# Attention block on one core: one split of the second weights moved ahead of the group mean, and a wait put ahead of GpSimd's first sums of rows

## The chip, the cores and the metric

One core of one Trainium2 chip runs one program. The metric is device microseconds of that core, the median of three runs. The profile that is read here is one further execution of the same program; times on the trace count from its first instruction.

## The reference, cut to what matters

The input x is (16, 512, 32, 32): 16 images of 512 channels and N = 1024 positions. For each image

```
h   = group_norm(x) * w + b             # 32 groups of 16 channels
q, k, v = split(qkv_w @ h + qkv_b)      # 512 x 1024 each
attn = softmax(q^T k / sqrt(512))       # 1024 x 1024
out  = x + out_w @ (attn v)^T + out_b
```

The kernel uses that q^T k = h^T (wq^T wk) h and that out_w v = (out_w wv) h. So two products of weights are made once, ahead of all images: G from wk and wq ("weights 0"), U from wv and the transposed out_w ("weights 1"). The biases become three vectors of weights: sums over rows of the weights, each row scaled by a bias.

## The kernel before, in words

All matrices are kept as two float32r parts: a high part, rounded by ScalarE, and a "rest" (the small part), the full value less the high part, made by VectorE. A product is three matmuls: high by high, high by rest, rest by high (lines 459 to 461 in the main part; 475, 482 and 484 for the products of weights). Each engine runs an order that is written out by hand, and engines meet at semaphores only; nothing is planned at run time. So an instruction that waits holds everything that stands behind it on its own engine.

After the start, 16 images follow one another, each with a T stage (G by h), the scores, a V stage (h by U) and the output. TensorE has work nearly without a gap. The change is in the start alone, the first 35 us or so:

- **SP's queue** issues the loads in this order: weights 0 in four blocks (each block is 128 rows of two matrices, two transfers of 256 KB), the first image in four transfers of 512 KB, the matrix `block_avg` for the group means, then weights 1 in four blocks (lines 344 to 356).
- **ScalarE** makes the high parts (`weight_part`, line 749) of weights 0, then scales the rows of weights 0 by the biases (`wq_wk_rows`, line 774), makes the high parts of blocks 0 and 1 of weights 1, copies G out of PSUM (`product_part`, line 754) and makes block 2's high part. Then it waits for the scale and bias of the group norm (`s_norm`, 8 steps) and makes the high parts of h for two channel tiles (line 757), block 3's high part, and the other two of h. Then come rows of weights 1 scaled (line 785), `first_full(2)` (line 761), which waits for the sum of the scaled rows (`s_rows_sum[0]`), two more rows, U out of PSUM, and `first_full(3)`, which also waits for TensorE's first two weight vectors.
- **VectorE** makes the rests (`weight_rest`, line 1216), the statistics of the first image (lines 1230, 1235), four small steps after the mean (lines 1239 to 1244), one step after the variance (line 1248), three steps that give scale and bias (lines 1252 to 1256), the rests of G and U (`product_rest`, line 1221), and h in full and its rests (lines 1316, 1264). Then follow the combined tiles of h, the key bias's dot products and the tiles of T (lines 1279 to 1373).
- **TensorE** runs the product of weights 0, six matmuls of zeros (line 504), the group mean (line 492), the first high by high part of weights 1 (three tiles; the fourth needs a bank that is still read), the variance (line 516, after VectorE's fourth small step), the low parts of block 0, and so on to block 3. Then comes the T stage, with the weight vectors (line 466) behind its first nine matmuls.
- **GpSimd** adds the scaled rows of weights 0 with accumulating transfers, SBUF to SBUF, 512 KB each: the even blocks (line 1109) and the odd blocks (line 1111) as soon as ScalarE has scaled them, then, behind the step for the reciprocal root of the variance (line 1121), the sum of both (line 1116). The same follows for weights 1.

At the start of the first image's scores, ScalarE makes the eight high parts of the T sums (line 834), of which the last two need VectorE's last T sums (line 1373, `first_sum(S4, kk)`), and then copies the first score tiles (`copy_first`, line 869). TensorE's second scores product waits for the first of these copies (`s_p1`).

Semaphores that matter: `s_w[w][k]` (block k of weights w landed, 32 for both transfers), `s_whi`, `s_wlo` (high part, rest made), `s_norm` (steps of the norm), `s_even`, `s_odd`, `s_rows_sum` (sums of rows).

Of the kernel before, what the change touches and what calls it, by code (L numbers as in the profile page):

```python
# [19 lines left out]
CT = C // P  # L20
# [3 lines left out]
DMA = 16  # L24
# [85 lines left out]
def attention_kernel(nc, x, wq, wk, wv, wo_t, cols, block_avg, out):  # L110
# [5 lines left out]
    with ctx:  # L116
# [3 lines left out]
        def sem(name):  # L120
            return ctx.enter_context(nc.semaphore(name))
# [75 lines left out]
        def g_rows(t, i):  # L197

            return t[:, i // 2:i // 2 + 3:2, i % 2, :]
# [65 lines left out]
        u_bank = [4, 5, 6, 3]  # L265
# [3 lines left out]
        s_w = [[sem(f"weights{w}_loaded{k}") for k in range(CT)] for w in range(2)]  # L269
# [59 lines left out]
        def lone_wait(eng, which, count):  # L329
            eng.wait_ge(which, count)  # L330
            eng.sem_inc(s_carrier, 1)
# [124 lines left out]
        def _(pe):  # L456
# [15 lines left out]
            def product_high(w, k, banks, tiles=range(CT)):  # L472
                pe.wait_ge(s_whi[w], k + 1)
                for i in tiles:
                    nc.tensor.matmul(ring[:, banks[i], :], w_hi[w][:, 2 * k, i * P:(i + 1) * P], w_hi[w][:, 2 * k + 1, :],
                                     start=k == 0, stop=False)

            def product_low(w, k, banks, tiles=range(CT)):
                pe.wait_ge(s_wlo[w], k + 1)
                for i in tiles:  # L480
                    cs = slice(i * P, (i + 1) * P)
                    nc.tensor.matmul(ring[:, banks[i], :], w_hi[w][:, 2 * k, cs], w_lo[w][:, 2 * k + 1, :],
                                     start=False, stop=False)
                    a = nc.tensor.matmul(ring[:, banks[i], :], w_lo[w][:, 2 * k, cs], w_hi[w][:, 2 * k + 1, :],
                                         start=False, stop=k == CT - 1)
                    if k == CT - 1:
                        a.then_inc(s_prod[w], 1)

            def first_mean():
                pe.wait_ge(s_avg, DMA)  # L490
                pe.wait_ge(s_aggr, CT)
                nc.tensor.matmul(ps_mean, avg[:, :], mv[:, :, 0], start=True, stop=True).then_inc(s_mean, 1)
# [8 lines left out]
            def zero_products(count):  # L501

                for _ in range(count):
                    nc.tensor.matmul(ring[:, 7, :], zeros[:, 0:P], zeros[:, 0:HALF], start=True, stop=True)
# [4 lines left out]
            for k in range(CT):  # L509
                product_high(0, k, g_bank)  # L510
                product_low(0, k, g_bank)
            zero_products(6)
            first_mean()
            product_high(1, 0, u_bank, range(CT - 1))
            pe.wait_ge(s_norm, 4)
            nc.tensor.matmul(ps_var, avg[:, :], spread[:, :], start=True, stop=True).then_inc(s_var, 1)
            product_low(1, 0, u_bank, range(CT - 1))
            product_high(1, 1, u_bank, range(CT - 1))

            pe.wait_ge(s_prod_lo[0], 1)  # L520
# [575 lines left out]
        def _(pool):  # L1096
# [5 lines left out]
            def rows(w, k):  # L1102
                return raw[0][:, 2 * k:2 * k + 2, :] if w == 0 else wo_rows[k][:, :]

            def add_rows(w):

                sides = 2 - w
                pool.wait_ge(s_rows[w], 2 * sides)
                nc.gpsimd.dma_start(rows(w, 2), rows(w, 0), accum_op=ALU.add).then_inc(s_even[w], DMA)
                pool.wait_ge(s_rows[w], 4 * sides)  # L1110
                nc.gpsimd.dma_start(rows(w, 3), rows(w, 1), accum_op=ALU.add).then_inc(s_odd[w], DMA)

            def sum_rows(w):
                pool.wait_ge(s_even[w], DMA)
                pool.wait_ge(s_odd[w], DMA)
                nc.gpsimd.dma_start(rows(w, 3), rows(w, 2), accum_op=ALU.add).then_inc(s_rows_sum[w], DMA)

            add_rows(0)
            pool.wait_ge(s_warm, 1)
            pool.wait_ge(s_norm, 5)  # L1120
# [84 lines left out]
        def _(dve):  # L1205
# [7 lines left out]
            def weight_rest(w, k):  # L1213
                dve.wait_ge(s_whi[w], k + 1)
                here = slice(2 * k, 2 * k + 2)
                nc.vector.tensor_tensor(w_lo[w][:, here, :], raw[w][:, here, :], w_hi[w][:, here, :].bitcast(FP32),
                                        ALU.subtract).then_inc(s_wlo[w], 1)

            def product_rest(w, i, dst_lo, dst_hi, src):
                dve.wait_ge(s_prod_hi[w], i + 1)  # L1220
                nc.vector.tensor_tensor(dst_lo, src, dst_hi.bitcast(FP32), ALU.subtract).then_inc(s_prod_lo[w], 1)

            def g_rest(i):
                product_rest(0, i, g_rows(g_lo, i), g_rows(g_hi, i), ring[:, g_bank[i], :].rearrange("p (a n) -> p a n", a=2))

            def stats_part(n, q):
                k, half = q // NB, q % NB
                if half == 0:
                    dve.wait_ge(s_x[k], (n + 1) * DMA)
                nc.vector.bn_stats(stats[:, k, half, :], xs[:, k, half * HALF:(half + 1) * HALF]).then_inc(s_stats, 1)  # L1230

            def first_stats_close():
                lone_wait(dve, s_stats, CT * NB)
                for k in range(CT):
                    nc.vector.bn_aggr(mv[:, k, :], stats[:, k, :, :].rearrange("p s e -> p (s e)")).then_inc(s_aggr, 1)

            def first_about_mean():
                dve.wait_ge(s_mean, 1)
                nc.vector.tensor_copy(gmean[:, :], ps_mean).then_inc(s_norm, 1)
                nc.vector.tensor_tensor(dmean[:, :], ps_mean, mv[:, :, 0], ALU.subtract).then_inc(s_norm, 1)  # L1240
                dve.wait_ge(s_norm, 2)
                nc.vector.tensor_tensor(shift[:, :], dmean[:, :], dmean[:, :], ALU.mult).then_inc(s_norm, 1)
                dve.wait_ge(s_norm, 3)
                nc.vector.tensor_tensor(spread[:, :], shift[:, :], mv[:, :, 1], ALU.add).then_inc(s_norm, 1)

            def first_variance():
                dve.wait_ge(s_var, 1)
                nc.vector.tensor_scalar(veps[:, :], ps_var, EPS, None, ALU.add).then_inc(s_norm, 1)
# [9 lines left out]
            def h_rest(n, k):  # L1258
                if n == 0:
                    dve.wait_ge(s_first[k], 1)  # L1260
                else:
                    dve.wait_ge(s_hf, (n - 1) * CT + k + 1)
                dve.wait_ge(s_hhi, n * CT + k + 1)
                nc.vector.tensor_tensor(h_lo[:, k, :], h_full[:, k, :], h_hi[:, k, :].bitcast(FP32),
                                        ALU.subtract).then_inc(s_hlo, 1)
# [45 lines left out]
            def first_full(k):  # L1311

                dve.wait_ge(s_even[0], DMA)
                dve.wait_ge(s_odd[0], DMA)
                dve.wait_ge(s_norm, NORM)
                nc.vector.tensor_scalar(h_full[:, k, :], xs[:, k, :], h_scale[:, k:k + 1], h_bias[:, k:k + 1],
                                        ALU.mult, ALU.add).then_inc(s_first[k], 1)
# [3 lines left out]
            for q in range(CT * NB):  # L1321
                stats_part(0, q)
            first_stats_close()
            first_about_mean()
            weight_rest(1, 0)
            first_variance()
            g_rest(0)
            weight_rest(1, 1)
            first_affine()
            weight_rest(1, 2)  # L1330
            for i in range(1, CT):
                g_rest(i)
            first_full(0)
            weight_rest(1, 3)
            h_rest(0, 0)
            first_full(1)
            h_rest(0, 1)
# [447 lines left out]
```

## Time and profile before

| | us |
|---|---|
| three runs | 1977.72, 1978.09, 1980.64 |
| median | 1978.09 |
| the profiled execution, its own time | 1979.92 |
| its span, first to last instruction | 1978.1 |
| TensorE busy in it | 1971.6 |
| VectorE, ScalarE, GpSimd busy | 1664.6, 1123.1, 448.0 |
| TensorE's granted clock, mean | 1.000 |

The own time of the profiled execution is 1.8 us longer than its span; the rest lies before the first and after the last instruction. TensorE's ends are modelled, so its busy time is a bound, not a proof that it worked at its peak.

### The profile page before, as it was taken

What the parts mean: (1) busy time and instruction counts of PE and PEld (TensorE: products, weight loads), DVE (VectorE), ACT (ScalarE), POOL (GpSimd) and SP (SyncE); (2) the same over time, 40 slices, a digit from 0 to 9 for tenths busy, and PEclk for the clock granted to TensorE, in tenths of its full rate; (3) what the DMA queues carried; (4) which work ended last, traced back from release to release, by engine and by line L of the source; (5) the groups of instructions that cost most, each with busy time, mean ns of one, the idle gap of its engine ahead of it and who ended that gap; (6) DMA issues with size and microseconds to landing.
All of it is one profiled execution on the core that took longest, in us unless ns stands there. A gap on an engine that the chain in (4) does not pass through costs nothing.

```text
span 1978.1 us, 26068 instructions
## 1 busy us (share of the span) xinstructions
PE 1971.6 (100%) x9894; PEld 1681.8 (85%) x9895; DVE 1664.6 (84%) x2010; ACT 1123.1 (57%) x1431; POOL 448.0 (23%) x306
## 2 busy tenths in 40 slices
PE   9999999999999999999999999999999999999999
PEld 7888888888888888888888888888888888888887
DVE  7897997969889798796988979788797988969866
ACT  6564646646465564645746466564664646556461
POOL 1112140221412213131231401214022131221311
PEclk9999999999999999999999999999999999999999
DMA  6305233051431604325043340424305143160411
GB/s 177 129 7 114 75 66 128 7 149 40 75 119 17 172 6 76 119 50 144 6 75 114 58 136 7 112 76 70 124 7 151 37 75 119 21 172 2 75 33 54
DMA packets 102636, 157.89 MB, mean 80 GB/s; under 512 B 49376, under 2 KB 51264, under 8 KB 102512
## 3 DMA queue, kind: packets, MB, share of 16 engines
q0 software_dynamic: 31264, 73.15, 17.1%
q1 hardware_dynamic: 71248, 83.08, 13.7%
q8 instruction: 79, 1.29, 0.3%
q14 instruction: 45, 0.37, 0.1%
HBM read 85.57 MB, written 68.26 MB: 78 GB/s over the span
## 4 chain that ended last, share of the span: by engine, by line
PE 88%; DVE 2%; ACT 1%; issue 0%; DMA 0%; SPq 0%; DVEq 0%; ACTq 0%
PE ring L459 29%; PE ring L460 29%; PE ring L461 29%; DVE stage L1438 0%; DVE stage L1457 0%; DVE run_max L1450 0%; DVE stats L1230 0%; ACT stage L881 0%; DVE stage L1506 0%; DMA u_dram<-r_lo 0%; DVE r_lo L1431 0%; ACT xs L888 0%; ACT ring L869 0%; ACT r_hi L863 0%; DVE u_lo L1518 0%
## 5 line engine op out<-in xcount | busy, mean ns | idle before, releaser
L459 PE MATMUL ring<-r_hi 128*128 128x512 f32 (+1 forms) x1724 | 656.6, 381 | 0.2 <-DVE r_lo L1477 0.2
L460 PE MATMUL ring<-r_lo,r_hi 128*128 128x512 f32 (+1 forms) x1724 | 656.4, 381 | 0.0
L461 PE MATMUL ring<-r_hi,r_lo 128*128 128x512 f32 (+1 forms) x1724 | 656.2, 381 | 0.0
L459 PEld LDWEIGHTS ring<-r_hi 128*128 128x128 f32 x1724 | 324.3, 188 | 62.1 <-DVE r_lo L1477 0.7
L461 PEld LDWEIGHTS ring<-r_hi,r_lo 128*128 128x128 f32 x1724 | 324.2, 188 | 62.1
L460 PEld LDWEIGHTS ring<-r_lo,r_hi 128*128 128x128 f32 x1724 | 324.3, 188 | 61.2
L881 ACT ACTIVATE stage<-ring,keybias 128x512 f32<-128x512 f32 x256 | 175.2, 685 | 164.2 <-PE ring L461 161.4
L1170 POOL PARTITION_ALL_REDUCE stage<-stage x32 | 127.2, 3976 | 466.5 <-DVE stage L1530 466.5
L854 ACT ACTIVATE stage<-ring,by_tile 128x512 f32<-128x512 f32 x120 | 82.5, 688 | 243.8 <-PE ring L461 243.8
L1462 DVE TENSOR_TENSOR r_lo<-stage,r_hi 128x1024 fp32r<-128x1024 f32 x128 | 182.2, 1453 | 0.0
L1450 DVE TENSOR_TENSOR run_max<-run_max,stage 128x512 f32<-128x512 f32 x192 | 132.0, 694 | 55.2 <-ACT stage L881 50.6
L459 PE MATMUL ring<-h_hi,r_hi 128*128 128x512 f32 x444 | 172.8, 389 | 0.1
L461 PE MATMUL ring<-h_hi,r_lo 128*128 128x512 f32 x444 | 172.7, 389 | 0.0
L460 PE MATMUL ring<-h_lo,r_hi 128*128 128x512 f32 x444 | 172.7, 389 | 0.0
L1457 DVE TENSOR_TENSOR stage<-stage,all_max 128x1024 f32<-128x1024 f32 x128 | 151.9, 1229 | 0.0
L900 ACT ACTIVATE stage<-stage 128x1024 f32<-128x1024 f32 x128 | 134.6, 1052 | 18.7 <-DVE stage L1457 18.7
L915 ACT ACTIVATE r_hi<-stage 128x1024 fp32r<-128x1024 f32 x128 | 135.9, 1061 | 2.8 <-DMA u_dram<-r_lo 0.3
L1165 POOL PARTITION_ALL_REDUCE all_max<-run_max x32 | 57.9, 1810 | 304.6 <-DVE run_max L1450 160.2
L761 ACT ACTIVATE stage<-xs,by_tile 128x1024 f32<-128x1024 f32 x62 | 76.5, 1233 | 83.6 <-DMA sum_row<-stage 82.6
L1230 DVE BATCH_NORM_STATS2 stats<-xs 128x6 f32<-128x512 f32 x128 | 80.6, 684 | 46.4 <-DMA xs<-x_in 46.4
L1406 DVE TENSOR_TENSOR stage<-stage,ring 128x512 f32<-128x512 f32 x90 | 60.6, 686 | 69.0 <-PE ring L461 58.9
L767 ACT ACTIVATE r_hi<-stage 128x1024 fp32r<-128x1024 f32 x64 | 68.0, 1063 | 76.8 <-DVE stage L1279 72.3
(199 smaller groups left out, 3924.5 us busy)
## 6 DMA issues: line engine op xcount, KB each, us to landing
xs<-x_in SPq DMA_DIRECT2D x64, 512.0 KB, 5.8
out<-xs SPq DMA_DIRECT2D x60, 512.0 KB, 2.7
out<-run_max POOLq DMA_DIRECT2D x60, 256.0 KB, 5.7
inv<-inv_row SPq DMA_DIRECT2D x32, 256.0 KB, 4.5
out<-spare POOLq DMA_DIRECT2D x30, 256.0 KB, 7.6
out<-all_max POOLq DMA_DIRECT2D x30, 256.0 KB, 5.0
r_hi<-g_dram POOLq DMA_DIRECT2D x15, 512.0 KB, 6.3
r_lo<-g_dram POOLq DMA_DIRECT2D x15, 512.0 KB, 5.7
```

The source lines that it names most:

```text
L459: nc.tensor.matmul(ps_out, st_hi, m_hi, start=first, stop=False, skip_group_check=goes_on)
L460: nc.tensor.matmul(ps_out, st_hi, m_lo, start=False, stop=False, skip_group_check=goes_on)
L461: return nc.tensor.matmul(ps_out, st_lo, m_hi, start=False, stop=last, skip_group_check=goes_on)
L854: nc.scalar.activation(stage[:, to + kk, :], ring[:, T_BANK[p] + kk, :], ACT.Identity, bias=t_bias[:, i:i + 1]).then_inc(done, 1)
L881: nc.scalar.activation(stage[:, to, :], ring[:, bank + i, :], ACT.Identity, bias=keybias[:, m:m + 1]).then_inc(done, 1)
L900: nc.scalar.activation(here, here, ACT.Exp, scale=SCALE).then_inc(s_exp, 1)
L915: nc.scalar.activation(p_pair(r_hi, b, nb, q), stage[:, 8 * nb + 2 * q:8 * nb + 2 * q + 2, :], ACT.Copy).then_inc(s_phi, 1)
L1170: nc.gpsimd.partition_all_reduce(stage[:, 8 * nb + 1, :], stage[:, 8 * nb, :], P, bass.bass_isa.ReduceOp.add).then_inc(s_allsum, 1)
L1230: nc.vector.bn_stats(stats[:, k, half, :], xs[:, k, half * HALF:(half + 1) * HALF]).then_inc(s_stats, 1)
L1450: nc.vector.tensor_tensor(run_max[nb][:, :], first, stage[:, 8 * nb + m, :], ALU.max).then_inc(s_rmax[nb], 1)
L1457: nc.vector.tensor_tensor(here, here, all_max[:, :].rearrange("p (o n) -> p o n", o=1).to_broadcast([P, 2, HALF]), ALU.subtract).then_inc( ...
L1462: nc.vector.tensor_tensor(p_pair(r_lo, b, nb, q), stage[:, 8 * nb + 2 * q:8 * nb + 2 * q + 2, :], p_pair(r_hi, b, nb, q).bitcast(FP32), AL ...
```

## The change

TensorE: two of six matmuls of zeros go; the low parts of block 0 of weights 1 are moved ahead of the wait for VectorE's fourth small step and of the variance. GpSimd: a wait for block 2 of weights 1 is put ahead of the first two sums of rows. VectorE: the rest of block 0 of weights 1 is moved ahead of the steps after the mean, the first rest of G ahead of the variance's step, and the rest of block 3 ahead of `first_full(0)`.

```
-            zero_products(6)
+            zero_products(4)
             first_mean()
             product_high(1, 0, u_bank, range(CT - 1))
+            product_low(1, 0, u_bank, range(CT - 1))
             pe.wait_ge(s_norm, 4)
             nc.tensor.matmul(ps_var, avg[:, :], spread[:, :], start=True, stop=True).then_inc(s_var, 1)
-            product_low(1, 0, u_bank, range(CT - 1))
             product_high(1, 1, u_bank, range(CT - 1))
...
+            pool.wait_ge(s_w[1][2], 2 * DMA)
             add_rows(0)
             pool.wait_ge(s_warm, 1)
             pool.wait_ge(s_norm, 5)
...
             first_stats_close()
+            weight_rest(1, 0)
             first_about_mean()
-            weight_rest(1, 0)
+            g_rest(0)
             first_variance()
-            g_rest(0)
             weight_rest(1, 1)
             first_affine()
             weight_rest(1, 2)
             for i in range(1, CT):
                 g_rest(i)
+            weight_rest(1, 3)
             first_full(0)
-            weight_rest(1, 3)
             h_rest(0, 0)
```

## Rows read from the trace of the kernel before

**Rows 1.** The page, busy us of each engine, share of the span, instructions.

```profile
PE 1971.6 (100%) x9894; PEld 1681.8 (85%) x9895; DVE 1664.6 (84%) x2010; ACT 1123.1 (57%) x1431; POOL 448.0 (23%) x306
```

**Rows 2.** Timeline of TensorE: start us, us, engine, line, op, tiles, count [idle before, releaser].

```profile
19.32 1.24 PE L504 MATMUL ring<-spare 128*128 128x512 bf16 x5
20.39 0.28 PE L492 MATMUL ring<-inv 128*128 128x4 f32 x2
20.54 0.96 PE L475 MATMUL ring<-r_hi 128*128 128x512 f32 x3
21.39 0.39 PE L516 MATMUL ring<-inv 128*128 128x4 f32 x2
22.53 0.50 PE L482 MATMUL ring<-r_lo,r_hi 128*128 128x512 f32 x1 [0.75 <-DVE r_lo L1216]
...
34.90 1.84 PE L466 MATMUL ring<-inv,stage 128*128 128x1 f32 x16
```

**Rows 3.** Timeline of VectorE, from the mean to the T sums.

```profile
20.71 0.16 DVE L1239 COPY inv<-ring 128x4 f32<-128x4 f32 x1 [2.70 <-PE ring L492]
...
21.26 1.22 DVE L1216 TENSOR_TENSOR r_lo<-stage,r_hi 128x1024 fp32r<-128x1024 f32 x1
22.39 0.15 DVE L1248 TENSOR_SCALAR inv<-ring 128x4 f32<-128x4 f32 x1
...
23.06 1.22 DVE L1216 TENSOR_TENSOR r_lo<-stage,r_hi 128x1024 fp32r<-128x1024 f32 x1
24.19 0.16 DVE L1252 TENSOR_TENSOR by_tile<-inv,col 128x4 f32<-128x4 f32 x1
...
28.31 1.22 DVE L1216 TENSOR_TENSOR r_lo<-stage,r_hi 128x1024 fp32r<-128x1024 f32 x1
...
38.11 1.23 DVE L1264 TENSOR_TENSOR h_lo<-stage,h_hi 128x1024 fp32r<-128x1024 f32 x1 [1.02 <-ACT stage L761]
...
60.37 1.41 DVE L1373 SCALAR_TENSOR_TENSOR stage<-ring,by_tile,stage 128x512 f32<-128x512 f32 x2
```

**Rows 4.** Timeline of ScalarE, from the second weights to the first score copies.

```profile
17.09 1.06 ACT L749 ACTIVATE r_hi<-stage 128x1024 fp32r<-128x1024 f32 x1 [0.76 <-DMA stage<-wo_t]
18.45 1.06 ACT L749 ACTIVATE r_hi<-stage 128x1024 fp32r<-128x1024 f32 x1 [0.30 <-DMA stage<-wo_t]
...
24.78 2.38 ACT L757 ACTIVATE h_hi<-xs,by_tile 128x1024 fp32r<-128x1024 f32 x2 [2.37 <-DVE by_tile L1256]
27.07 1.04 ACT L749 ACTIVATE r_hi<-stage 128x1024 fp32r<-128x1024 f32 x1
...
31.50 1.23 ACT L761 ACTIVATE stage<-xs,by_tile 128x1024 f32<-128x1024 f32 x1
...
36.84 1.24 ACT L761 ACTIVATE stage<-xs,by_tile 128x1024 f32<-128x1024 f32 x1 [0.96 <-PE ring L466]
...
62.37 2.04 ACT L869 ACTIVATE ring<-ring 128x512 f32<-128x512 f32 x4
```

**Rows 5.** Timeline of GpSimd.

```profile
9.21 0.19 POOL L1100 TENSOR_TENSOR inv<-by_tile 128x4 f32<-128x4 f32 x1 [8.38 <-issue]
...
22.70 1.06 POOL L1121 TENSOR_TENSOR inv<-inv,by_tile 128x4 f32<-128x4 f32 x1 [5.19 <-DVE inv L1248]
26.08 0.91 POOL L1116 DMA_DIRECT2D stage<-stage  x1 [2.32 <-DMA stage<-stage]
```

**Rows 6.** DMA issues from 10.1 to 11.05 us: size, us to landing.

```profile
stage<-wo_t SPq DMA_DIRECT2D x1, 256.0 KB, 10.6
```

**Rows 7.** DMA issues from 26 to 27 us: the last sum of rows.

```profile
stage<-stage POOLq DMA_DIRECT2D x1, 512.0 KB, 4.6
```

**Rows 8.** Windows: us, busy (count) of PE, PEld, DVE, ACT, POOL, granted clock, DMA share, GB/s.

```profile
14.20:19.20 5.00, 5.00 (x23) 3.96 (x23) 3.67 (x10) 3.94 (x6) 2.04 (x2) 1.00 1.06 379
19.20:24.20 5.00, 4.18 (x20) 2.89 (x19) 3.42 (x9) 3.21 (x6) 1.06 (x1) 1.00 1.06 223
```

**Rows 9.** Timeline of TensorE's weight loads at the second scores product.

```profile
63.07 0.19 PEld L459 LDWEIGHTS ring<-h_hi,r_hi 128*128 128x128 f32 x1 [0.47 <-DVE r_lo L1379]
```

More of the change, by code:

```diff
@@ L511, in _ @@
                 product_low(0, k, g_bank)
-            zero_products(6)
+            zero_products(4)
             first_mean()
             product_high(1, 0, u_bank, range(CT - 1))
+            product_low(1, 0, u_bank, range(CT - 1))
             pe.wait_ge(s_norm, 4)
             nc.tensor.matmul(ps_var, avg[:, :], spread[:, :], start=True, stop=True).then_inc(s_var, 1)
-            product_low(1, 0, u_bank, range(CT - 1))
             product_high(1, 1, u_bank, range(CT - 1))
@@ L1116, in sum_rows @@
                 nc.gpsimd.dma_start(rows(w, 3), rows(w, 2), accum_op=ALU.add).then_inc(s_rows_sum[w], DMA)
+            pool.wait_ge(s_w[1][2], 2 * DMA)
             add_rows(0)
@@ L1323, in _ @@
             first_stats_close()
+            weight_rest(1, 0)
             first_about_mean()
-            weight_rest(1, 0)
+            g_rest(0)
             first_variance()
-            g_rest(0)
             weight_rest(1, 1)
@@ L1332, in _ @@
                 g_rest(i)
+            weight_rest(1, 3)
             first_full(0)
-            weight_rest(1, 3)
             h_rest(0, 0)
```

## The prediction

> **What bounds the kernel now.** The page comes first: TensorE is busy 1971.6 us [rows 1] of a span of 1978.1, so the time can only fall by idle time or by work that leaves TensorE, and only where TensorE, followed to the end, starts everything earlier. The change touches the start alone, so I read the start engine by engine. TensorE's timeline [rows 2] has one place worth having: the six matmuls of zeros (five records; the sixth is missing, they run from 19.09 to 20.37, so 0.213 each), the mean at 20.39, three matmuls from 20.54, the variance at 21.39, and the first low part only at 22.53, released by VectorE's rest of block 0. VectorE [rows 3] sat idle 2.70 us for the mean, from 18.0 to 20.71, and made that rest at 21.26, after the mean's steps, though ScalarE had the high part at 18.15 (17.09 and 1.06) [rows 4]. The order is the cause, not the work.
>
> The next question is where a gain could be lost again. ScalarE waits 2.37 us for the scale and bias, to 24.78; GpSimd's root (22.70, 1.06 us) is part of that chain [rows 4, 5]. Then ScalarE runs without idle time to `first_full(3)` at 36.84, which waited 0.96 us for the weight vectors, started at 34.90; VectorE waited for it to 38.11 and has no idle time from there to 60.37 and beyond [rows 2 to 4]. Its last T sums there release ScalarE's last high part and the copy at 62.37, and TensorE's weight load at 63.07 stood 0.47 us [rows 9]. The row names line 1379, which TensorE doesn't wait for in the code; the wait that the code has is on the copy of 62.37. This is the second place that decides: TensorE's gain in the first 35 us is cut there to what ScalarE and VectorE gain.
>
> **TensorE, part by part.** A 512-column matmul costs 0.227: 23 of them touch 5.0 us, 22 pitches [rows 8].
> - Two zeros fewer: 2 x 0.213 = 0.43. The mean moves from 20.39 to 19.96. Its input is ready at 18.0, so no wait opens.
> - The low parts of block 0, six matmuls, follow the three high ones: 20.11 + 9 x 0.227 = 22.15. Their rest is made at 18.2 to 19.4 (VectorE is idle then), in time and ahead of the mean. The variance comes behind them at 22.15, where its input is ready at about 20.9, and takes about 0.15 like the mean. So the 0.17 of waiting at 21.22 to 21.39, the 1.0 from there to 22.53, and about 0.1 of restart go. The gain behind the variance is 0.43 + 0.17 + 1.0 + 0.1 = 1.7.
> - The seven matmuls to block 1's low parts end at 22.30 + 7 x 0.227 = 23.89 (the bank they need is free: the first rest of G now ends at 21.5). The weights want to load at 23.66.
>
> **VectorE and the norm.** The copy of the mean follows TensorE's row by 0.32, so the variance is read at 22.15 + 0.32 = 22.47, against 22.39 [rows 2, 3]: hardly moved, because before it stood behind the rest of block 0. The rest of block 1 starts at 22.55 and not at 23.06, and is seen at 23.8, where TensorE wants it at 23.66; the restart hides all but 0.03. The root starts 0.31 after the variance, at 22.78, and ends at 23.84 [rows 5]. Before, the three affine steps began at 24.19 since VectorE was busy until then; now it is free at 23.7 and the root ends it: about 24.0. **So the norm's end, and ScalarE from 24.78 on, gain only 0.2** (bounds 0.05 to 0.3, by how soon VectorE sees the root, which no row shows).
>
> Block 3's high part on ScalarE goes from 27.07 to 26.88, and its rest starts when that is done, at 27.97 and not 28.31, since `first_full(0)` no longer stands ahead. It is seen at 29.24; TensorE wants it at 29.14, and again the restart hides it. Without this edit TensorE would have stood 0.4 or more. Price on VectorE: the rests of h for tiles 0 to 2 come some 0.4 later at first, 31.1 for tile 0, where TensorE wants 30.95: under 0.05. The product of weights 1 ends near 31.2, and the weight vectors stand at 33.25 against 34.90, a gain of 1.65.
>
> **The second place.** `first_full(3)` needs the vectors (36.84 - 1.65 = 35.2) and ScalarE's own queue: it stood idle 0.96 before 36.84, and as neighbours overlap by some 0.1 it could have started at 35.74, now 35.55. So it gains 1.29, not 1.65. VectorE's own queue gives the same (its copies behind U's rests end at 36.8). VectorE goes from 38.11 to 36.8 and carries 1.3 through to 60.37; TensorE's third k step wants this rest at about 38.95 and gets it at 38.1. ScalarE's last high part there is due by VectorE's sum, not by its own queue, so TensorE is released at 63.07 - 1.3. Behind that point everything depends on work that moved by 1.3, and is carried along.
>
> **GpSimd's wait.** Behind it stand both sums, the root, the last sum, then all of GpSimd. Before, block 2 of weights 1 landed at 21.2 (issued at 10.6 and 10.6 more) [rows 6], beside sums that were issued as soon as ScalarE had scaled the rows (it was through at 16.33, 0.76 ahead of 17.09 [rows 4]). Blocks 0 and 1 came at 17.09 and 18.45 [rows 4], so block 2 is at most 1.36 later, 19.8, if nothing delays it; taking out the sums' bytes until then (I estimate 0.28 MB at 379 GB/s, 0.7 us [rows 8]) gives 19.1. Bounds: 18.3, and 21.2 as before. For the release I allow 0.5, and about 1 us for each issue like the 0.91 of 26.08 [rows 5]: 19.6 to 21.7, ahead of the root's 22.78, so the root pays nothing. The last sum took 4.6 to land [rows 7]; its 0.52 MB at 223 GB/s [rows 8] are 2.35 of that, 2.25 lie before and behind. Both sums are 1.05 MB, 4.7 us: landed at 19.6 + 4.7 + 2.25 = 26.5. The last sum is issued at about 26.8, where it was 26.08, and lands at 31.4. ScalarE wants it at 31.3 (31.50 - 0.2) [rows 4], TensorE at 33.25. Price 0.1, bounds 0 and 2.2. What it gives back: block 3, due on ScalarE at 26.9, has slack either way. I value the wait at nothing for TensorE.
>
> By the Trainium skill (DMA: Bandwidth & Descriptors, Anatomy of one DMA, SWDGE path) a transfer costs 2.0 us and its bytes at 436 GB/s, an estimate of 3.2 us for 512 KB; the row says 4.6 [rows 7], and by the page the last sum would land near 30 with no price at all.
>
> **Sum.** -1.3 + 0.1 = -1.2 us. Against the profiled execution's own 1979.92 this is 1978.7. That execution is 1.8 above the median of the runs; the same sum on the median 1978.09 gives **1976.9**.
>
> **The rivals.**
> 1. *Slower: GpSimd's wait ends late.* For: block 2 did land at 21.2, and nothing in the profile proves that the sums caused it. Then the sums are issued at 21.7 to 23.8, the root ends near 24.8 (affine steps 0.7 later than before), both sums land at 28.6, and the last sum lands at 33.5. ScalarE's `first_full(2)` goes to 33.5 (+2.0), `first_full(3)` to 37.7, and VectorE's chain and TensorE at 63.07 by +0.9: 1979.0. It decides from a last sum later than about 32.6, that is block 2 after 20.3. Against: DMA moved 379 GB/s while three blocks of weights and both sums shared it.
> 2. *The sums slip by half a microsecond or so*, block 2 near 19.7: 32.0, gain cut to 0.6: 1977.5.
> 3. *The root is held by VectorE.* Now it would start 0.23 into a rest of two SBUF inputs (22.55 to 23.77); before it began beside a rest of G that reads PSUM. The same engine's 128x4 add took 0.19 at 9.21, the root 1.06 [rows 5], so part of it may already be such waiting, or the power itself. If held to 23.77, the root ends at 24.8, the affine steps are 0.7 later than before, and TensorE stands 1.0 for block 3's rest; `first_full(3)` goes to 36.44: gain 0.4, 1977.7. The Trainium skill has this rule (SBUF — State Buffer, Who interferes with whom: a VectorE instruction with two SBUF inputs contends with a GpSimd one that reads SBUF, and the first issued holds the shared port). Before, the root ended at 23.76 beside such an instruction from 23.06, but had begun first, so the trace doesn't contradict it.
> 4. *Nothing binds at 63.07*: VectorE's chain has slack that I don't see, and TensorE carries 1.65: 1976.4.
> 5. *The change doesn't do what it says*: the wait doesn't speed blocks 2 and 3, which have slack anyway. Same time as my forecast.
>
> **How the numbers follow.** A measurement of this kernel can tell about 0.2%, 4 us, from no change; three equal runs of before spread over 2.9. Chances: forecast (with rival 5) 0.60, slip 0.13, root held 0.11, slower by 0.9 us 0.08, 1.65 carried 0.08. The range takes in 1976.4 and 1979.0 and about 1 us of scatter below and 0.5 above: 1975.4 to 1979.5. Every case lies within 4 us, so faster by over 0.2% gets 0.03, slower 0.03, what is left 0.94; these small chances stand for something not thought of, such as a lower granted clock, of which the profile shows none (1.00 in both windows [rows 8]).
>
> **What the profile after would show.** Mean at 19.96; rest of block 0 at 18.2 on VectorE; no TensorE idle before line 482; variance read at 22.5; affine steps at 24.0; block 3's rest at 28.0; weight vectors at 33.25; last sum issued near 26.8 and `first_full(2)` at 31.3 to 31.5; `first_full(3)` at 35.6; the copy of 62.37 at 61.1 and the weight load of 63.07 at 61.8, still with idle time before it. I am wrong if affine steps start after 24.5 (rival 3), if `first_full(2)` waits for DMA by more than 0.5 (rivals 1, 2), or if the load of 63.07 comes at 61.4 (rival 4).

## The result, and the profile after

The change made the kernel slower: 1981.24 us (median of 22 runs) against 1978.16 (22 runs), ratio 1.0015, interval 1.001 to 1.0021. That is 3.1 us, outside my range, and clear of noise: with this many runs the measurement tells about 1 us, not the 4 us that the prediction allowed it. One run of each kernel took far longer (2166.11 before, 4020.49 after) and is left out of the ratio. The profiled execution took 1981.37, span 1979.6. So the spans of the two profiles (1978.1 and 1979.6) differ by 1.5 only, and half of the loss is not in them. The first experiment finds the other half.

VectorE's timeline of the kernel after, where it answers to [rows 3]:

```profile
18.14 1.22 DVE L1217 TENSOR_TENSOR r_lo<-stage,r_hi 128x1024 fp32r<-128x1024 f32 x1 [0.15 <-ACT r_hi L749]
19.28 0.15 DVE L1240 COPY inv<-ring 128x4 f32<-128x4 f32 x1
...
21.22 0.16 DVE L1249 TENSOR_SCALAR inv<-ring 128x4 f32<-128x4 f32 x1 [0.56 <-PE ring L517]
21.30 1.21 DVE L1217 TENSOR_TENSOR r_lo<-stage,r_hi 128x1024 fp32r<-128x1024 f32 x1
23.47 0.16 DVE L1253 TENSOR_TENSOR by_tile<-inv,col 128x4 f32<-128x4 f32 x1 [0.96 <-POOL inv L1122]
...
28.99 0.81 DVE L1317 TENSOR_SCALAR stage<-xs,by_tile 128x1024 f32<-128x1024 f32 x1 [0.34 <-DMA stage<-stage]
...
39.61 1.23 DVE L1265 TENSOR_TENSOR h_lo<-stage,h_hi 128x1024 fp32r<-128x1024 f32 x1
```

The rest of block 0 stands where the change puts it, at 18.14, and the affine steps begin at 23.47, earlier than the 24.19 of [rows 3]. But the rest of h's last tile, 38.11 there, is at 39.61: +1.5, as the span.

ScalarE's and GpSimd's timelines after, answering to [rows 4] and [rows 5]:

```profile
24.06 2.38 ACT L757 ACTIVATE h_hi<-xs,by_tile 128x1024 fp32r<-128x1024 f32 x2 [1.71 <-DVE by_tile L1257]
...
34.05 1.24 ACT L761 ACTIVATE stage<-xs,by_tile 128x1024 f32<-128x1024 f32 x1 [3.17 <-DMA stage<-stage]
...
38.33 1.25 ACT L761 ACTIVATE stage<-xs,by_tile 128x1024 f32<-128x1024 f32 x1
...
20.07 1.18 POOL L1109 DMA_DIRECT2D stage<-stage  x1 [10.59 <-DMA stage<-wo_t]
20.96 1.20 POOL L1111 DMA_DIRECT2D stage<-stage  x1
21.54 1.90 POOL L1122 TENSOR_TENSOR inv<-inv,by_tile 128x4 f32<-128x4 f32 x1
29.43 0.92 POOL L1116 DMA_DIRECT2D stage<-stage  x1 [5.99 <-DMA stage<-stage]
```

The loss of this profile starts in two rows. The last sum of rows is issued at 29.43, not 26.08, and `first_full(2)` stands 3.17 us for it, to 34.05, which is 2.55 later than in [rows 4]. U's copies and `first_full(3)` stand behind it in ScalarE's queue, and VectorE behind those. The wait of 0.96 that stood ahead of `first_full(3)` before, and about 0.1 of overlap, take up part of it; what is left is the 1.5 of `first_full(3)` (38.33 against 36.84).

The DMA issues of the two first sums after (the even sum, then the odd one), and the DMA by windows with the columns of [rows 8]. The last two numbers of such a line are the busy share of the DMA engines and GB/s:

```profile
stage<-stage POOLq DMA_DIRECT2D x1, 512.0 KB, 4.9
...
stage<-stage POOLq DMA_DIRECT2D x1, 512.0 KB, 7.9
```

```profile
20.00:22.00 2.00, 2.00 (x11) 1.70 (x10) 1.44 (x3) 2.00 (x4) 1.94 (x3) 1.00 0.19 39
22.00:24.00 2.00, 2.00 (x10) 1.60 (x10) 0.98 (x5) 0.35 (x1) 1.44 (x2) 1.00 1.06 197
24.00:26.00 2.00, 2.00 (x11) 1.64 (x10) 2.00 (x4) 1.94 (x2) 0.00 (x0) 1.00 1.03 199
26.00:28.00 2.00, 2.00 (x9) 1.39 (x8) 1.54 (x3) 2.00 (x3) 0.00 (x0) 1.00 0.55 102
```

The even sum landed at 20.07 + 4.9 = 25.0, the odd one at 20.96 + 7.9 = 28.9. Between the last load and the first bytes of the sums the DMA engines were nearly idle: their share was 0.19 from 20 to 22 us, and 0.00 from 20.5 to 21.5. The sums alone moved 198 GB/s. Two more profiles below show the same 2 us, first the kernel before, run once more, then the kernel after with the wait on block 1; there the engines had no gap:

```profile
20.00:22.00 2.00, 1.25 (x5) 1.05 (x6) 2.00 (x4) 2.00 (x4) 1.06 (x1) 1.00 1.05 241
```

```profile
20.00:22.00 2.00, 2.00 (x12) 1.66 (x11) 1.45 (x3) 2.00 (x4) 1.27 (x2) 1.00 0.98 198
```

TensorE after, answering to [rows 2], and the windows in which its granted clock (the third number from the end) isn't 1.00:

```profile
18.13 0.36 PE L492 MATMUL ring<-inv 128*128 128x4 f32 x2
18.34 0.95 PE L475 MATMUL ring<-r_hi 128*128 128x512 f32 x3
19.41 0.50 PE L482 MATMUL ring<-r_lo,r_hi 128*128 128x512 f32 x1
...
20.91 0.28 PE L517 MATMUL ring<-inv 128*128 128x4 f32 x2
...
34.16 1.92 PE L466 MATMUL ring<-inv,stage 128*128 128x1 f32 x16 [0.66 <-DMA stage<-stage]
...
37.18 0.59 PE L461 MATMUL ring<-h_hi,g_lo 128*128 128x512 f32 x1
37.57 0.63 PE L459 MATMUL ring<-h_hi,g_hi 128*128 128x512 f32 x1
```

```profile
36.00:38.00 2.00, 2.00 (x9) 1.59 (x9) 1.52 (x3) 2.00 (x5) 0.86 (x1) 0.80 0.00 0
38.00:40.00 2.00, 2.00 (x6) 1.62 (x5) 2.00 (x6) 1.58 (x2) 0.00 (x0) 0.50 0.76 131
40.00:42.00 2.00, 2.00 (x9) 1.54 (x9) 1.98 (x2) 0.00 (x0) 0.86 (x1) 0.84 0.01 4
```

The mean is at 18.13, not at the 19.96 that I forecast; line 482 still starts about 0.4 late (at 19.41, where three matmuls from 18.34 end at 19.0), since the rest of block 0 is made from 18.14 to 19.36. TensorE stands for the last sum too (0.66), and behind that wait the granted clock falls to half (1.2 GHz) for some three microseconds. At the second scores product TensorE stood again for the copies, 0.59 us, so this half clock seems to have cost nothing at the end; the wait alone, below, lost as much at full clock.

### The profile page after: what moved, and what is told of

It is laid out like the page before. It is cut to its first block, busy times and chain, and to the rows that moved or that the text cites. A ratio compares the mean times of both kernels' runs of the same rounds, so it can differ in the third digit from the quotient of the medians.

```text
span 1979.6 us, 26065 instructions
## 1 busy us (share of the span) xinstructions
PE 1972.5 (100%) x9892; PEld 1680.9 (85%) x9893; DVE 1666.5 (84%) x2010; ACT 1123.3 (57%) x1431; POOL 448.7 (23%) x306
## 4 chain that ended last, share of the span: by engine, by line
PE 88%; DVE 2%; ACT 1%; issue 0%; DMA 0%; SPq 0%; DVEq 0%; ACTq 0%
PE ring L459 29%; PE ring L461 29%; PE ring L460 29%; DVE stage L1439 0%; DVE stage L1458 0%; DVE run_max L1451 0%; DVE stats L1231 0%; ACT stage L881 0%; DVE stage L1507 0%; DMA u_dram<-r_lo 0%; DVE r_lo L1432 0%; ACT xs L888 0%; ACT ring L869 0%; ACT r_hi L863 0%; DVE u_lo L1519 0%
## 5 line engine op out<-in xcount | busy, mean ns | idle before, releaser
L900 ACT ACTIVATE stage<-stage 128x1024 f32<-128x1024 f32 x128 | 134.6, 1052 | 18.6 <-DVE stage L1458 18.6
L915 ACT ACTIVATE r_hi<-stage 128x1024 fp32r<-128x1024 f32 x128 | 135.8, 1061 | 2.8 <-DMA u_dram<-r_lo 0.3
L1151 POOL DMA_DIRECT2D r_hi<-u_dram x15 | 8.6, 572 | 457.4 <-PE ring L461 457.4
```

Of the source, the lines that this page charges most:

```text
L900: nc.scalar.activation(here, here, ACT.Exp, scale=SCALE).then_inc(s_exp, 1)
L915: nc.scalar.activation(p_pair(r_hi, b, nb, q), stage[:, 8 * nb + 2 * q:8 * nb + 2 * q + 2, :], ACT.Copy).then_inc(s_phi, 1)
```

## The experiments

Each time is a median of 10 or 11 runs, beside the kernel before on the same chip. Ratios have intervals of about 0.0009 either way, so the traces carry the finer differences.

**The kernel before, once more.** No edit.

> The kernel before once more, unchanged, for a second profile of it. Theory 1 (the profiled execution of before was not the typical one: TensorE ran at 1.2 GHz to 10.4 us there): the typical execution is at 2.4 GHz from about 7 us, the product of the first weights ends near 17 us, the mean is at about 18.3, the last sum of rows is issued at 26 and lands at 30.7, and ScalarE's first_full(2) waits for it. Span about 1976.4, time 1978.2. Rival: the profile of before was typical and the 1.8 us lie outside the span; then the mean is at 20.4 again.

1978.13 us, ratio 1.0 (0.9991 to 1.0009), span 1976.5. VectorE, ScalarE and GpSimd in this profile:

```profile
21.28 1.21 DVE L1216 TENSOR_TENSOR r_lo<-stage,r_hi 128x1024 fp32r<-128x1024 f32 x1
22.41 0.15 DVE L1252 TENSOR_TENSOR by_tile<-inv,col 128x4 f32<-128x4 f32 x1
...
36.49 1.23 DVE L1264 TENSOR_TENSOR h_lo<-stage,h_hi 128x1024 fp32r<-128x1024 f32 x1
...
30.92 1.25 ACT L761 ACTIVATE stage<-xs,by_tile 128x1024 f32<-128x1024 f32 x1 [0.38 <-DMA stage<-stage]
...
14.01 1.17 POOL L1109 DMA_DIRECT2D stage<-stage  x1 [4.18 <-ACT stage L774]
16.43 0.87 POOL L1111 DMA_DIRECT2D stage<-stage  x1 [1.25 <-ACT stage L774]
20.92 1.06 POOL L1121 TENSOR_TENSOR inv<-inv,by_tile 128x4 f32<-128x4 f32 x1 [3.62 <-DVE inv L1248]
26.32 0.92 POOL L1116 DMA_DIRECT2D stage<-stage  x1 [4.34 <-DMA stage<-stage]
```

The profile that I predicted from was not the typical execution. Here are two of its rows of TensorE, in the product of the first weights, and below them two rows from the same stretch of the profile after:

```profile
7.84 0.63 PE L482 MATMUL ring<-r_lo,r_hi 128*128 128x512 f32 x1
8.27 0.63 PE L484 MATMUL ring<-r_hi,r_lo 128*128 128x512 f32 x1
```

```profile
7.21 0.40 PE L484 MATMUL ring<-r_hi,r_lo 128*128 128x512 f32 x1
7.45 0.40 PE L482 MATMUL ring<-r_lo,r_hi 128*128 128x512 f32 x1
```

There TensorE went at the pace of the 1.2 GHz level (0.43 a matmul) up to 10.4 us, though the granted clock of that stretch reads 1.00; in the others it goes at 0.23 from 7 us or so on. So the mean was 1.8 us late there (20.39 against 18.6), and the weight vectors too (34.90 against 33.12), while the last sum was not (issued at 26.08 and 26.32). This delay hid that ScalarE is bound by the last sum: typically `first_full(2)` waits for it, 0.38 us, to 30.92. In [rows 4] it started at 31.50 without a wait. From here on, "typical" means this second profile.

**The change without GpSimd's wait.**

```
-            pool.wait_ge(s_w[1][2], 2 * DMA)
             add_rows(0)
```

> The kernel after without GpSimd's wait; both new orders of TensorE and VectorE stay. Theory 1 (the 3 us are the wait's: it delays the sums of rows, and ScalarE and VectorE with them): last sum issued near 26.1, landed 30.7, time as before, 1978.2 (ratio 0.9995 to 1.0003), since the last sum binds ScalarE in before too. Rival 2 (the new orders cost, by the root held beside the rest of block 1, or by the restart of TensorE): 1979.5 or more. My prediction's sum, if nothing of the sums bound: 1977.

1978.14, ratio 0.9999 (0.9991 to 1.0008), span 1976.4; last sum issued at 26.22, `first_full(2)` at 30.83. The new orders of TensorE and VectorE neither gain nor cost anything that these runs can tell; what TensorE gains ends at the same sum (`first_full(2)` waits 0.23 for it). Two rows of TensorE at block 3:

```profile
27.16 1.20 PE L475 MATMUL ring<-r_hi 128*128 128x512 f32 x4
28.42 0.50 PE L482 MATMUL ring<-r_lo,r_hi 128*128 128x512 f32 x1
```

TensorE reached block 1's high part 1.48 us sooner than in the typical before (20.76 against 22.24), but this block's low part only 0.85 sooner (28.42 against 29.27): it waited for the high part and for the rest, both behind the norm.

**The wait alone, in the kernel before.**

```
+            pool.wait_ge(s_w[1][2], 2 * DMA)
             add_rows(0)
```

> The kernel before with GpSimd's wait alone. Theory 1: as slow as after, 1981.2 (ratio 1.0013 to 1.0018), last sum issued near 29.4 and landed near 34.0. Rival 2 (the orders cost): 1978.2 to 1979.

1981.03, ratio 1.0015 (1.0006 to 1.0023), span 1979.2; last sum issued at 29.09, `first_full(2)` at 33.72. The wait is the whole loss, within the interval. The clock stayed at 1.00 in every window to 41 us of this profile, so the half clock of the profile after isn't the cause either.

**The wait on another block.** First block 1, as in the diff, then block 3, in place of block 2.

```
-            pool.wait_ge(s_w[1][2], 2 * DMA)
+            pool.wait_ge(s_w[1][1], 2 * DMA)
```

> The kernel after with the wait on block 1 of the second weights, not block 2. Block 1 landed near 18.4, block 2 near 19.9. Theory 1: the sums are issued 1.5 us earlier, so about half of the loss comes back: 1979.7 (1979.2 to 1980.3). Rival 2: no change against after, 1981.2. A third possibility, that the sums' landing is set by the DMA engines and not by the issue: 1981.2 too, with the odd sum landing at 28.9 again.

1978.95, ratio 1.0003 (0.9994 to 1.0012), span 1977.3.

> The kernel after with the wait on block 3 of the second weights, the last load, in place of block 2. So far first_full(2) on ScalarE starts with the landing of the last sum: 30.8 us without a wait, 31.8 with block 1, 34.0 with block 2, and the span follows it one for one. Theory 1: block 3 lands about 1.1 later than block 2, the sums and the span come 0.5 to 1.3 later: 1982.3. Rival (the loss has another cause, such as the half clock seen in after): 1981.2, as after.

1982.31, ratio 1.0021 (1.0012 to 1.003), span 1980.5. With these the loss follows the place of the wait (the last column is what is left of the span after VectorE begins the rest of h's last tile):

| kernel | even sum issued | last sum issued | `first_full(2)` | rest of h's last tile | span | span less that rest |
|---|---|---|---|---|---|---|
| before, typical | 14.01 | 26.32 | 30.92 | 36.49 | 1976.5 | 1940.0 |
| wait on block 1 | 18.59 | 27.19 | 31.80 | 37.37 | 1977.3 | 1939.9 |
| wait alone, block 2 | 19.74 | 29.09 | 33.72 | 39.28 | 1979.2 | 1939.9 |
| after, block 2 | 20.07 | 29.43 | 34.05 | 39.61 | 1979.6 | 1940.0 |
| wait on block 3 | 20.96 | 30.33 | 34.96 | 40.52 | 1980.5 | 1940.0 |

The kernel ends 1939.9 to 1940.0 us after VectorE begins this rest in every profile of this study; the first profile of before (38.11, 1978.1) has the same. Block 1 cost less than I expected: the even sum started 4.6 us later, and the last sum was issued 0.9 later. In the typical before the first two sums were in flight for 8.6 and 9.4 us, beside the loads; issued at 18.59 and 19.48 they took 4.9 and 7.2, and the DMA engines went from the loads to the sums with hardly a gap. From block 1 to the kernel after the even sum's issue moves by 1.48 and the last sum by 2.24, and from there to block 3 both move by 0.9, while the engines stand idle in between (from 20.5 to 22.5 us for block 3). Starting the sums late costs little as long as the engines stay busy, and one for one or more behind the loads.

**The queue behind the sum.** The kernel after, with the work behind `first_full(2)` moved ahead of it:

```
             wo_rows_part(2)
-            first_full(2)
             wo_rows_part(1)
             wo_rows_part(3)
             for i in range(CT):
                 product_part(1, i, u_hi[:, i, :], ring[:, u_bank[i], :])
+            first_full(2)
             first_full(3)
...
             h_rest(0, 1)
-            h_rest(0, 2)
             for i in range(CT):
                 product_rest(1, i, u_lo[:, i, :], u_hi[:, i, :], ring[:, u_bank[i], :])
+            h_rest(0, 2)
```

> The kernel after, with the two rows of weights and U's four copies on ScalarE ahead of first_full(2), and U's four rests on VectorE ahead of the rest of h's third tile. Theory 1 (the price is what stands behind first_full(2) in ScalarE's queue while it waits for the last sum): ScalarE works through its wait, first_full(3) starts near 36.0 in place of 38.3, and most of the loss comes back: 1978.5 to 1979.3. Rival (TensorE's own waits and its half clock in after make the 3 us): 1981.0.

The profile did about as expected: span 1977.1, `first_full(3)` at 35.90, now waiting for TensorE's vectors, and VectorE's rest at 37.17.

```profile
33.77 1.24 ACT L761 ACTIVATE stage<-xs,by_tile 128x1024 f32<-128x1024 f32 x1
35.90 1.24 ACT L761 ACTIVATE stage<-xs,by_tile 128x1024 f32<-128x1024 f32 x1 [0.89 <-PE ring L466]
```

The median did not: 1980.84, ratio 1.0013 (1.0004 to 1.0022), which is the rival's number. The eleven runs fall in two groups. Four with a mean granted clock of 1.000 took 1978.9 to 1979.75; seven with 0.998 or 0.999 took 1980.68 to 1982.05. The profiled one is the fastest of the first group. So the expected size about holds for runs at full clock, and a lower clock goes with 1.5 us more by the medians of the groups (1980.89 against 1979.36). In the kernel after, runs with 1.000 and 0.999 took the same time, so there ScalarE may hide it. No trace shows an execution of the second group; that its clock fell at the same place as in the profile after is inferred, and what makes it fall stays open: the profile here has the same waits of TensorE as the one of after (0.46 and 0.66 against 0.41 and 0.66) and kept the full clock.

**The same moves in the kernel before.** The diff is the same.

> The kernel before with the same two moves. In its typical execution first_full(2) waits 0.38 for the sum, VectorE 0.77 and 0.48 behind it. Theory 1: a gain of 0.4 to 0.6 us, 1977.6. Rival (TensorE needs the rest of h's third tile sooner than it comes): 1978.5 or more.

1978.14, ratio 0.9999 (0.999 to 1.0008), span 1976.6: no gain, against my theory. `first_full(2)` no longer waits, but `first_full(3)` now stands 0.50 for TensorE's vectors, and VectorE's rest is at 36.56 as before. The next limit was right behind, about as early as the old one.

**The root beside another instruction.** The change without the wait, and

```
-            g_rest(0)
             first_variance()
+            g_rest(0)
             weight_rest(1, 1)
```

> The kernel after without GpSimd's wait, and on VectorE the first rest of G behind the variance's step again, so that this rest, which reads PSUM, and not block 1's, which reads SBUF twice, stands beside the root on GpSimd. Theory (the root is held by a VectorE instruction that began earlier and reads SBUF twice): the root takes 1.06 us and not 1.90, the affine steps start near 22.5. Rival (it is slow because of the descriptors that GpSimd writes at the time): 1.9 again. Time 1978.1 either way, as the last sum still binds.

Time 1977.96, ratio 0.9999 (0.999 to 1.0008), span 1975.8; the affine steps began at 22.54, as expected. That span is 0.7 under the typical one, but the last sum bound here too (`first_full(2)` waited 0.28); in this execution it was issued at 25.73, 0.6 sooner, as the first sums started 0.3 sooner and flew 0.4 us less. The median shows 0.2, inside the interval. The root in three kernels: without the wait (with VectorE's rest of block 1 ahead of it), this one, and the wait alone on before:

```profile
21.02 1.22 DVE L1216 TENSOR_TENSOR r_lo<-stage,r_hi 128x1024 fp32r<-128x1024 f32 x1
21.26 1.90 POOL L1121 TENSOR_TENSOR inv<-inv,by_tile 128x4 f32<-128x4 f32 x1 [4.07 <-DVE inv L1248]
```

```profile
21.05 1.06 POOL L1121 TENSOR_TENSOR inv<-inv,by_tile 128x4 f32<-128x4 f32 x1 [4.02 <-DVE inv L1248]
```

```profile
21.20 1.98 POOL L1122 TENSOR_TENSOR inv<-inv,by_tile 128x4 f32<-128x4 f32 x1
```

Where VectorE's rest of block 1 began before the root, the root ended 0.91 to 0.93 after that rest's end: 23.16 against 22.24 without the wait, 23.18 against 22.27 with the wait alone, 23.44 against 22.51 in after. Where the root began first, it took 1.06. In the first of the three GpSimd issued no transfer near it (the last at 16.32), so the descriptors aren't the cause there. This is the rule of the Trainium skill (SBUF — State Buffer, Who interferes with whom: a VectorE instruction with two SBUF inputs and a GpSimd one that reads SBUF contend, whoever issues first has the port for the whole instruction). For the root behind the rest these traces agree with it. They show no sign of the other direction: the rest that began at 21.28 in the typical before, 0.36 into the root, took 1.21 as elsewhere.

The run with the wait on block 3 shows a second way to a long root, which I had not looked for:

```profile
20.92 1.22 DVE L1217 TENSOR_TENSOR r_lo<-stage,r_hi 128x1024 fp32r<-128x1024 f32 x1
...
21.85 1.20 POOL L1111 DMA_DIRECT2D stage<-stage  x1
22.42 1.72 POOL L1122 TENSOR_TENSOR inv<-inv,by_tile 128x4 f32<-128x4 f32 x1
```

Here VectorE's rest was over at 22.14, before the root's row begins, and VectorE did nothing beside it. The root ended at 24.14, that is 1.09 after the end of the odd sum's issue (23.05), about the 1.06 of a root by itself. So GpSimd's own issue of a transfer can lengthen the root's row as well; the rival of this experiment falls for the kernel without the wait, not everywhere.

**Both together.** The kernel of the root's experiment and the two moves of U.

> The kernel of the run before it in this study (no wait of GpSimd's, the root not held) with U's copies and rests ahead of first_full(2) and of the rest of h's third tile. With the two moves alone on before, first_full(3) waited 0.50 for TensorE's vectors; the new order of TensorE brings these 1.0 sooner. Theory 1 (ScalarE's queue behind the sum and TensorE's vectors bind by turns, so only both moves together gain): first_full(3) near 34.3, VectorE's rest of h's last tile near 35.5 against 36.5 in before, time 1977.2 to 1977.5. Rival (something else binds VectorE at 36): 1978.1.

1977.39 (1977.16 to 1977.92) against 1978.12, ratio 0.9997 (0.9988 to 1.0006), span 1975.6. ("The run before it" in the text is the root's experiment.) VectorE's rest is at 35.65, 0.84 before the typical kernel before, and it waits for nothing there. But the profile of the root's experiment had this rest at 35.89 already, in an execution that was early by itself, so between these two traces the moves of U are worth only 0.24. The medians say 0.7 less than the kernel before; the interval of the ratio doesn't exclude none. It is the version with the lowest median of this study.

**A wait ahead of the odd sum alone.** The root's kernel, with the wait between the two sums.

```
                 pool.wait_ge(s_rows[w], 4 * sides)
+                if w == 0:
+                    pool.wait_ge(s_w[1][2], 2 * DMA)
```

> The same kernel without the moves of U, and with the wait on block 2 of the second weights ahead of the odd sum alone; the even sum starts as in before. Theory 1 (what counts is when the second of both sums lands, and two sums issued one behind the other after the loads take 8.9 us): even sum landed near 21, odd sum alone takes 4.9 from 19.9, last sum issued near 25.3 to 25.8, time 1977.7 to 1978.1. Rival (any wait for block 2 costs as in after, since the odd sum then has the same late issue): last sum issued near 29, 1981.

1978.9, ratio 1.0003 (0.9994 to 1.0012), span 1976.7. GpSimd in it:

```profile
20.85 0.87 POOL L1113 DMA_DIRECT2D stage<-stage  x1 [6.00 <-DMA stage<-wo_t]
21.42 2.05 POOL L1123 TENSOR_TENSOR inv<-inv,by_tile 128x4 f32<-128x4 f32 x1
26.50 0.91 POOL L1118 DMA_DIRECT2D stage<-stage  x1 [3.03 <-DMA stage<-stage]
```

The odd sum, issued at 20.85 as late as in after, landed in 5.1 us, and the last sum is issued at 26.50, near the 26.32 of the typical before: the rival falls. It is later than the 25.3 to 25.8 that I expected, since block 2 landed later beside the even sum and released the odd one at 20.85, not 19.9. The root queues behind the odd sum's issue, starts after VectorE's rest of block 1 and takes 2.05, but this cost nothing here: `first_full(2)` still waited 0.19 for the sum, to 31.11. Why the median is 0.8 above before, where this profile (of one of the fastest runs, 1978.44) is 0.2 above, stays open.

## Why the prediction was wrong

**The step that failed is the price of GpSimd's wait**, 0.1 us in my sum. By the runs the wait costs 2.9 alone and 3.1 with the rest. Block 2 landed at 19.7 (issued at 10.4 and 9.3 more), between my 19.1 and the 20.3 from which I said slower; the mistake is behind it. I took both sums as landed at 19.6 + 4.7 + 2.25 = 26.5. They landed at 28.9: issued 0.5 later than forecast; at 198 GB/s and not 223, because my rate came from a window that still held the tail of a load; and with 3.5 us before and behind the bytes, not 2.25. First came 1.7 us from issue to first bytes, in which the engines idled; at the end the bulk of the bytes was through near 27.1, a trickle of 8 to 16 GB/s ran on to 28.5, and the sum landed at 28.9. Why the odd sum trails so far stays open; the other lone or first sums landed after 4.9 and 5.1 us. I compared 26.8 with 26.08 and looked at the total of bytes, which is the same; what counts is that in before the sums ran inside the loads' time (block 3 of weights 1 landed only at 25.9 in the typical before, at 20.9 in after), and here almost none of them did. With `first_full(2)` at 34.05 in place of my 31.3 the price is 2.7, and my own sum gives -1.3 + 2.7 = +1.4, where the two spans differ by 1.5.

**The base was wrong too.** I took one profile for the kernel, though it was 1.8 us above the median and I had written that down as an offset. It was a different execution: TensorE slow to 10.4 us, hence 0.8 us of slack at `first_full(2)` (31.50 against a sum landed at 30.7) that the typical execution doesn't have, as it waits 0.38. In it the other edits may have gained my 1.3; no run can test this, since that execution doesn't come back. On the typical one they gain nothing (1978.14 without the wait).

By the steps of the prediction:
- *TensorE's own gain:* in sign right. The weight vectors, which TensorE starts behind its first nine matmuls of T, gained 0.5 without the wait (32.63 against 33.12 in the typical before) and 1.0 with the root not held either (32.12, in an execution that was some 0.3 early by itself), not 1.65. The sum part by part was near at first (1.48 at block 1's high part, where I had 1.7), and failed behind it. TensorE then waits for block 3's high part and rest, which come after the norm; with the root not held it doesn't, but its weight loads wait 0.49 for the first rest of G and 0.38 for block 1's rest instead.
- *Affine steps:* wrong term. I had the root at 1.06 and them 0.2 sooner; the root took 1.90 and they came 0.78 later than typical (23.19 against 22.41, without the wait). Rival 3, at 0.11, was true as a mechanism and right in size (I wrote that held, the steps come 0.7 later than before). It cost no time because the sum binds, so its 1977.7 was wrong.
- *Block 3's rest moved ahead:* useful, and for a reason that I hadn't seen. The wait alone, which lacks this move, has TensorE standing 1.46 us for this rest (at 30.65), since `first_full(0)` ahead of it waits for the sums; the kernel after has no wait of that length. My 0.4 for it without GpSimd's wait was not tested.
- *The second place:* right. TensorE's weight load stood at the second scores product in every trace (0.47 to 1.72 us), and all work behind it is carried along: the constant 1940.0 us.
- *Rival 1, slower:* right in its place (the last sum, `first_full(2)`, `first_full(3)`), wrong in its condition and price. It needed no late block 2, and it measured 1.5 against the execution that I read, 3.1 against the typical one, where I gave 0.9.
- *Range and chances:* the range ended at 1979.5. The change of 0.16% lies inside the 0.2% to which I gave 0.94, but it is a real loss, which that bound hides.

## What to carry to other kernels

Before costing an edit, see that the profiled execution is the typical one; if it is off the median by more than the effect looked for, find what differs in it before reading slack from it. A transfer that is held back until others have landed leaves the DMA engines idle in between: price it from its own issue to its landing with nothing beside it, and set that against what waits for it. After a gain, name the next thing in the same queue: here the sum and TensorE's vectors bound by turns, and no single move gained anything clear of noise.

## What the runs showed of the hardware

- Two accumulating SBUF-to-SBUF transfers of 512 KB, issued 0.9 us apart on idle DMA engines, took 8.8 us together (20.07 to 28.9) at 198 GB/s; with loads and sums in flight together (14.2 to 19.2 us of the two profiles of before) the engines moved 369 to 379 GB/s in all. The Trainium skill (DMA: Bandwidth & Descriptors, Anatomy of one DMA, SWDGE path) gives 2.0 us and the bytes at 436 GB/s, an estimate of 3.2 us for one; the rows say 4.6 to 5.1.
- A 128x4 operation on GpSimd took 1.06 us when it began ahead of a VectorE instruction with two SBUF inputs, and 1.90 to 2.05 when it began during one, ending 0.91 to 0.93 after it. Behind GpSimd's own issue of a transfer, with no VectorE instruction beside it, it took 1.72.
- TensorE's clock fell to 1.2 GHz from about 37.3 to 40.6 us in the profile after, behind waits of 0.41 and 0.66 us and sixteen one-column matmuls; the profile with U's work moved ahead, with waits of 0.46 and 0.66 and the same matmuls, and the one of the wait alone, with a wait of 1.46, kept 2.4 GHz. And in the first profile of before a pace of 0.43 us a matmul stood beside a granted clock of 1.00 up to 10.4 us.
